# The causal mask of the second attention's mixing: four products over 32 rows instead of one over 128

## The reference, cut to what matters

```python
def _L1_attn_ref(hidden_states, W_attn, b_attn, P_q, P_k, P_v, W_back, W_proj, b_proj):
    B, S, D, DC, H = (4, 512, 192, 96, 12)
    HD = DC // H
    ...
    qh, kh, vh = (split(q), split(k), split(v))
    scores = jnp.einsum('bhqd,bhkd->bhqk', qh, kh) / jnp.sqrt(jnp.float32(HD))
    causal = jnp.tril(jnp.ones((s, s), dtype=scores.dtype))
    scores = scores * causal + -10000.0 * (1.0 - causal)
    weights = jax.nn.softmax(scores, axis=-1)
    ctx = jnp.einsum('bhqk,bhkd->bhqd', weights, vh)
```

## Time and profile before

| what | value |
|---|---|
| median of three runs | 980.3 us |
| the profiled execution, its span | 980.29 us, 978.3 us |
| outside the span | 1.99 us |
| TensorE busy | 724.6 us (74%) |
| weight loads busy (beside the products) | 523.7 us (54%) |
| VectorE, ScalarE, GpSimd busy | 647.4, 641.1, 345.1 us |
| granted TensorE clock, mean | 0.814 of 2.4 GHz |
| the mixing block | from 672.9 to 726.3 us |

### The profile page before, as it was taken

How to read it: one execution, slowest core, us unless ns; L and a number is a source line. 1 busy time by engine, 2 the same in 40 slices (tenths; PEclk the granted TensorE clock), 3 DMA queues, 4 the chain that set the end, 5 groups by cost and what they waited for, 6 DMA issues and landing times. The chain is left out here.

```text
span 978.3 us, 18613 instructions
## 1 busy us (share of the span) xinstructions
PE 724.6 (74%) x6846; PEld 523.7 (54%) x6847; DVE 647.4 (66%) x1350; ACT 641.1 (66%) x1217; POOL 345.1 (35%) x266
## 2 busy tenths in 40 slices
PE   2684661442597838999998559787995998999984
PEld 2552330221476424599998425332453576999984
DVE  3488989999598888755544376884139783545442
ACT  1568947999697858865554349565754753666763
POOL 6720820000000000357776344363003003677753
PEclk9797555555699667999999869756996998999998
DMA  6446770000121319624333256483006832333332
GB/s 193 138 86 190 212 227 10 8 17 0 52 97 50 118 57 312 203 47 64 57 56 47 42 220 227 146 301 131 2 2 239 304 114 65 43 58 60 52 49 25
DMA packets 61394, 105.67 MB, mean 108 GB/s; under 512 B 9705, under 2 KB 43196, under 8 KB 61068
## 3 DMA queue, kind: packets, MB, share of 16 engines
q1 hardware_dynamic: 44940, 88.21, 27.2%
q0 software_dynamic: 16384, 16.53, 10.9%
HBM read 76.84 MB, written 27.87 MB: 107 GB/s over the span
## 5 line engine op out<-in xcount | busy, mean ns | idle before, releaser
L2383 DVE COPY m_xgT<-m_px 128x768 f16<-128x768 f16 (+1 forms) x46 | 22.9, 497 | 121.4 <-PE m_px L2228 121.4
L2350 ACT ACTIVATE m_pu<-m_pu,m_b,m_unit 128x256 f32<-128x256 f32 (+1 forms) x138 | 63.9, 508 | 59.8 <-PE m_pu L2260 58.4
L1140 ACT ACTIVATE a_ex<-m_pieces,a_nb 128x256 bf16<-128x256 f16 x192 | 94.3, 497 | 5.4 <-DVE a_nb L1166 5.4
L2391 DVE SCALAR_TENSOR_TENSOR m_hT<-m_pu,m_unit,m_hT 128x512 f16<-128x512 f32 (+1 forms) x138 | 85.9, 663 | 16.2 <-ACT m_hT L2343 15.9
L977 PE MATMUL a_pp<-a_room 16*128 16x256 bf16 x240 | 56.1, 412 | 39.6 <-DVE m_pieces L1154 31.8
L2354 ACT ACTIVATE m_pu<-m_pu,m_unit 128x512 f32<-128x512 f32 (+1 forms) x69 | 41.2, 597 | 61.9 <-PE m_pu L2260 61.6
L2343 ACT ACTIVATE m_hT<-m_pu,m_unit 128x512 f16<-128x512 f32 (+1 forms) x138 | 81.5, 635 | 0.0
L2194 POOL DMA_INDIRECT m_xg<-xn_d,m_token x70 | 69.8, 998 | 31.8 <-issue 20.6
L2202 POOL DMA_INDIRECT out_h<-m_yo,m_token x39 | 62.1, 1593 | 41.9 <-DVE m_yo L2401 18.6
L2202 POOL DMA_INDIRECT h_d<-m_yo,m_token x39 | 62.1, 1591 | 37.1 <-DVE m_yo L2401 19.5
L2260 PE MATMUL m_pu<-m_xgT,m_w 128*128 128x256 f16 (+1 forms) x690 | 71.1, 263 | 1.3 <-DVE m_xgT L2383 1.3
(11 more groups left out here) (492 smaller groups left out, 1775.4 us busy)
## 6 DMA issues: line engine op xcount, KB each, us to landing
m_pieces<-in_m_w SPq DMA_DIRECT2D x11, 768.0 KB, 5.2
a_early_w<-in_m_w SPq DMA_DIRECT2D x10, 768.0 KB, 5.3
hv_raw<-in_m_w SPq DMA_DIRECT2D x8, 768.0 KB, 6.0
w1h_d<-hv_parts SPq DMA_DIRECT2D x8, 768.0 KB, 4.1
m_w<-w1h_d SPq DMA_DIRECT2D x8, 768.0 KB, 9.7
m_pieces<-in_m_w SPq DMA_DIRECT2D x8, 576.0 KB, 6.1
a_room<-in_m_w SPq DMA_DIRECT2D x8, 576.0 KB, 3.7
hv_raw<-in_m_w SPq DMA_DIRECT2D x8, 576.0 KB, 5.8
```

The costliest lines, as they stand in the source:

```text
L1140: last = act.activation(ex[:, n % 2, r], v16t[:, n, r, :], ACT.Exp, bias=nbt[:, n, r:r + 1], scale=scale, accum_out=sumst[:, n, r:r + 1])
L2350: act.activation(pu[:, u, n, q * w:(q + 1) * w], pu[:, u, n, q * w:(q + 1) * w], ACT.Relu, bias=b1[:, bass.ds(e * FC + 2 * n + q, 1)], sca ...
L2391: last = v.scalar_tensor_tensor(hT[:, u, 1, third], pu[:, u, n, 0:2 * w], unit[:, 1:2], hT[:, u, 0, third], ALU.mult, ALU.subtract)
```

## The change

The mask of mixing was one product per head over 128 rows: the identity as weights, the mask as the moving operand of 2 x 128 columns. It becomes four products per head over 32 rows, in the group of rows where the head's own queries and keys lie. Product b has 32 rows of the mask (its 128 columns as weights) and moves the 32 x 32 identity twice (2 x 32 columns), into columns 32b to 32b + 31 of both diagonal blocks. The loop has b outside and the head inside. Each head needs the rows of the mask in its own partitions, so the tile `mask` has a copy of each 32 rows in all four groups: five planes of 128 x 128 instead of two. The first plane, used by the maxima, stays.

```diff
-        self.mask = c.sb("a1_mask", [P, 2, P], BF16, ctx)
+        self.mask = c.sb("a1_mask", [P, 5, P], BF16, ctx)
...
-                            for hh in range(HG):
-                                last = nc.tensor.matmul(diagonal(pb[:, j, hh]), c.identb[:], both(1),
-                                                        start=False, stop=True)
+                            for b in range(4):
+                                for hh in range(HG):
+                                    r0 = 32 * ((HG * (n % UNITS) + hh) % 4)
+                                    last = nc.tensor.matmul(
+                                        diagonal(pb[:, j, hh])[:, :, 32 * b:32 * (b + 1)], mask[r0:r0 + 32, 1 + b, :],
+                                        c.identb[r0:r0 + 32, r0:r0 + 32].unsqueeze(1).to_broadcast([32, 2, 32]),
+                                        start=False, stop=(b == 3))
                             last.then_inc(scored, 1)
...
-    f["mask"] = np.stack([future, future.T], 1).astype(bfloat16)
+    by_column = [np.tile(future[32 * b:32 * (b + 1)], (4, 1)) for b in range(4)]
+    f["mask"] = np.stack([future, *by_column], 1).astype(bfloat16)
```

More of the change, by code:

```diff
@@ L3046, in diagonal @@
                     return bank.rearrange("p (x c) -> p x c", c=S)[:, :, 0:P]
-                def both(major):
-                    return mask[:, major:major + 1, :].to_broadcast([P, 2, P])
+                masks = mask[:, 0:1, :].to_broadcast([P, 2, P])
                 with ExitStack() as s3:
@@ L3131, in score @@
                                 for hh in range(4):
-                                    last = nc.tensor.matmul(diagonal(pa[:, j, hh]), c.identb[:], both(0),
+                                    last = nc.tensor.matmul(diagonal(pa[:, j, hh]), c.identb[:], masks,
                                                             start=False, stop=True)
```

## The result

The changed kernel takes 963.61 us (median of four runs, 962.77 to 964.96) against 980.14 for before (four runs, 979.33 to 981.95): a ratio of 0.9841, 95% interval 0.9815 to 0.9867. Forecast were 971.3, in 968.8 to 976.3. The profiled execution took 963.23 us, its span 961.5.

The account below looks back on a forecast made before the run. The prediction took TensorE to bound mixing, with ScalarE next. Full-clock scores save 28 x 0.29 = 8.1 us; with the half-clock start 9.0 in all, so 980.29 - 9.0 = 971.3 us, range 968.8 to 976.3.

Parts of the forecast that it names:

- TensorE sets the pace, ScalarE next: In mixing, TensorE bounds a unit of 1.49 us; after the change 1.20 us, still above ScalarE's 1.13.
- The groups run beside each other, and a passage goes: In mixing's mask part, row groups overlap and the 0.09 us array-shape switch between QK and mask disappears.
- The step of three mask products: In mixing, three mask products, one per row group, take 36 ns; four such steps make 0.144 us per score.
- The first four units: Mixing's first four scores run at half clock, each taking 0.65 us after instead of 1.19; a little under 1.0 us gained.
- Feeding: Rival: TensorE gets instructions too slowly, 61 ns per product, a unit takes 1.83 us, the kernel 988.9 us; chance 0.06.
- The mask's load and scaling cost nothing: Ahead of mixing, the load grows from 64 to 160 KB, scaling by at most 0.5 us, covered by 0.9 us.
- The rest moves up whole: Behind mixing, work shifts earlier without new waits; its clock, against work moved 9 us, gives or takes about 1 us.
- The reference: The time of before that the forecast subtracts from: 980.29 us, its profiled execution taken as the median of the runs, 980.3.

Follow-up runs that it names:

- e6: The changed kernel with its twelve mask products each over all 128 rows, the full identity as weights: 976.09 us.
- e1: The kernel before with only the mask's tile, load and scaling widened to five planes, products unchanged: 980.37 us, ratio to before 1.0006.
- e4: The changed kernel with the new mask products in units 16 to 31 only, the old ones in units 0 to 15: 973.08 us.
- e5: The changed kernel with the mask's two loops exchanged, so a head's four products stand behind one another: 965.69 us.
- e8: The kernel before, run again with no edit: 979.97 us, ten runs from 975.68 to 982.96.
- e3: The changed kernel with each image's two transposes in mixing done seven times over: 976.62 us.
- e11: The changed kernel with 96 products of 16 columns and their loads added heading the query and key projection, where TensorE waits anyway: 964.86 us.
- e13: The kernel before with 32 products of 16 columns and 32 loads added where TensorE waits anyway: 976.01 us, ratio 0.9989.
- e7: The changed kernel with each image's two transposes in mixing done twice: 970.10 us.

## Why the prediction was wrong

- **TensorE sets the pace, ScalarE next:** right. A unit went from 1.49 to 1.18 us against 1.20 forecast, 0.05 above ScalarE's 1.13.
- **The groups run beside each other, and a passage goes:** right, and shown by e6, which has the same twelve products without the groups and gains nothing.
- **The step of three mask products:** 36 ns were taken, 30 measured (0.10 us for the twelve, three steps and the stagger). The work of `score` takes 0.39, not 0.42; 28 units by 0.024 are 0.7 us, and mixing gave 9.7 to 9.8 where 9.0 were forecast.
- **The first four units:** `score` at half clock takes 0.65 (674.00 to 674.65), as worked out, and the clock rises at the same place of the stage (679.5 before, 678.4 after, and mixing starts 1.0 earlier).
- **Feeding:** 30 products and 30 loads go through in 1.18 us, 39 ns per product, far under the 61 of rows 10. The Trainium skill, "TensorE: Matmul & The Clock Gate", names about 62 ns per product for decoding in software (the part on the 56 ns) and 107 ns for a load of 128 columns (section LDWEIGHTS). Neither binds in this trace: a product takes 39 ns, and four loads in one group start within 0.13 us.
- **The mask's load and scaling cost nothing:** right as far as e1 can tell (within 3 us); the scaling grew from 0.34 to 0.44 us, where 0.5 more was allowed for.
- **"The rest moves up whole", its clock giving or taking about 1 us:** this step failed. In the two profiles compared the rest behind mixing gave 6.2 us, and 1.0 more lies ahead of it; with mixing's 0.7 that is what the profile after has over the forecast. Of the 6.2, routing's 2.0 are one half-clock stretch; the last experts' 4.2 are about 1.9 for the other and about 1.9 for the last scatters' gap. Over the later series, where before's median is 976 to 979.5 and after's 964.6, all that is not mixing is about 3. The bound of 1 us had been set beside a row of a stretch at 0.66 without working out what one more stretch at half clock costs. With two of them at 2.0 and 1.9 us it should have been some 4 us; the gap between scatters had no term at all.
- **The reference:** three or four runs of before within 2 us looked like a narrow kernel. It spreads over 14 us (973.6 to 987.8 in 24 runs), the changed one over 4 in eight runs (962.8 to 966.4), and the half-changed e4 over 11 in nine. The forecast started from the one at 980.3, some 3 to 4 us above the medians of three of the four later series.

Open stays why before's executions spread and after's less. The granted clock goes with it in part: of the 69 executions of before in the four series, the fourteen under 976 us were granted 0.823 in the mean, the 26 over 979 us 0.819. What decides where a half-clock stretch falls is not shown. The part of the code fetches is seen in the scatters' gap but not in the times. A kernel faster than after did not come out of the experiments.

## What to carry to other kernels

A product over all 128 rows that stands between products over 32 rows cost here the columns of all three heads in a row and one passage of the array (0.43 us); given the same row groups as its neighbours it ran beside itself, even though that needed four times as many instructions and copies of the operand. Check by a variant with the same instruction count but full rows. And bound what moves behind a shortened stage by what one more half-clock stretch costs there, and take the spread of the reference from more than a handful of runs.

## What the runs showed of the hardware

- Products over different groups of 32 rows overlap even when those of one group stand together in the code (e5): twelve in 0.12 us.
- Twelve products of 64 columns over 128 rows cost 0.45 us with the passage, three of 256 cost 0.43 (e6): 128-column weights for every 64 columns are all but hidden.
- A stretch of 3.4 us at half clock more cost 2.0 us in routing (four profiles of fifteen), 1.9 in the last experts (e4) and 1.1 in an output stage that was granted 0.87 instead of 1.00 (e4, e7). The same instructions had it in one execution and not in another (before and e8 against e1).
- With a 16 KB packet of code starting 0.2 to 1.6 us after the last gather, the next scatter came 1.3 to 1.9 us later in the profile than after's 4.35 (before, e1, e3, e8, e11). 64 to 192 instructions more on TensorE some 390 us earlier moved the packet there (e11) or away (e13); no difference in the median followed.
